# Loading the first chunk of x and base_w ahead of everything else, with the base products started from it, in a two-layer mixer kernel

## The chip, the cores and the metric

The kernel runs on one core of a Trainium2 chip. The metric is the device time of one launch in microseconds (us), as the median over several runs.

## The reference

The input x has 64 samples of 32 channels and 512 positions, float32. Two layers are applied, each one a mix over channels followed by a product along the positions, with the input of the layer added to its result. Cut to what matters for the change:

```python
def layer0(x, cond):                       # x: 64 x 32 x 512, cond: 64 x 128
    h = gelu(cond @ W0 + b0)
    h = gelu(h @ W1 + b1)
    att = softmax(h @ W2 + b2)             # 64 x 8, the mixing network
    agg_w = einsum('bk,koi->boi', att, weight)      # one 32 x 32 matrix per sample
    y = einsum('boi,bih->boh', agg_w, x) + (att @ bias_k)[:, :, None]
    w = softmax of the two largest of (y @ gate_w.T), 0 elsewhere     # 8 experts
    low = einsum('bsd,erd->ebsr', y, lora_A)
    return x + y @ base_w.T + base_b + 2 * einsum('ebsr,eor,bse->bso', low, lora_B, w)

def layer1(x, cond):                       # a grouped convolution of 9 taps, then
    ...                                    # 4 experts, the two best by a router
```

The kernel uses that the mixing matrix and the product along positions act on different axes: it computes x @ base_w.T, x @ lora_A.T and x @ gate_w.T first (they need no mixing matrix) and mixes the products of each tile afterwards.

## The kernel before

**Tiles.** The 64 samples times 32 channels are 2048 rows. They form G = 4 groups of TG = 4 tiles of 128 rows (4 samples each). The 512 positions are DC = 4 chunks of 128; x is stored transposed, so a chunk of x is a 128 x 512 tile `xT_s[:, g % 2, c, :]`, and `wT_s[:, c, :]` (kept in the memory of `x1T`) is the same chunk of base_w.

**Float32 as two parts.** The large products are made in the type fp32r. A tile is split into a high part (ScalarE, ACT: `x_high` L513, `base_high` L598) and a low part, the tile minus its high part. For group 0 and base_w the low parts are VectorE's (DVE: `x_low`, `base_low`, both by `minus` L788), for groups 1 to 3 GpSimd's (POOL: `x_low` L371). `hi_lo` (L1099 to L1101) then makes three products for each pair of chunks: high by high, high by low, low by high.

**Products on TensorE (PE).** `x_base(0, t, chunks)` is x @ base_w.T of tile t of group 0, 3 matmuls of 512 columns for each chunk, added up in the PSUM bank `P0[t]`; all four tiles have a bank of their own. A chunk can be used when its `x_lo` and `base_lo` are there. `x_logits(c)` (L1112) is x @ [lora_A, gate_w] of group 0 in plain float32, four tiles, from the weights `lgw_s`. For groups 1 to 3 `x_first(g, t)` makes these logits and the first 128 columns of the base product in one, 3 matmuls of 264 columns for each chunk.

**Head.** All engines follow an order written out by hand. PE first runs filler products `keep_busy(4, n)` (L1092: n matmuls of 256 columns of ones), then the mixing network in small float32 products (h1 L1338, h2 L1342, the logits of the softmax L1344 and L1347), with more filler between them while ACT makes each gelu (L603, L608) and the exponential (L611). DVE makes the softmax (L947 to L952). PE turns it round (`attT` L1351) and spreads it over tiles (`attb` L1354); `mix_sum` (DVE L792, L796) makes the mixing matrices of a group from `attb` and the weights `wrep_s`, ACT places them into `mixT` (`mix_place` L593), and `mixb` (L1360) gives the bias.

**Routing of group 0.** `mix_logits(0, t)` (PE L1129) mixes the logits of a tile. DVE adds the bias (`logits` L820), then `route0(0)` ranks 8 gates with eleven small operations (`gates`, L768 to L782: `top`, `eq`, `above`, `dif`, `rank`, `kept`, `tot`, `inv`, `w`) and weighs the expert products (`lw` L828). ACT makes the exponential in it (`gate_exp` L556), as soon as `dif` is there; behind it in ACT's order stand `lb_h` (L634, the high part of lora_B) and the four copies `p0_out(0, t)` (L534) that take the base products of group 0 out of PSUM. `x_first(1, t)` writes to the same PSUM bank as `x_base(0, t)` and waits for that copy (`p0_ok`). `turn_lw(0)` (PE L1172) transposes `lw`. Then `make_y(0)` (L1191, `bias_row` L1203, `experts0`) brings the parts of the layer together, and DVE adds them up (L849, L855) into `x1T`.

**Loads.** SP issues early_s (cond, W0, W1, W2, the biases and bias_k), lgw_s, then for each chunk x and base_w of group 0, then group 1 and the rest. ACT issues wrep_s (the mixing weights). POOL's `x_low(1, 2)` waits for `lb_lo`, which DVE gives when it has made the low part of lora_B, behind route0(0).

From there each group's routing, layer 1 of the group before and the products of the next group are interleaved in the same way.

## Time and profile before

| | us |
|---|---|
| median of 3 runs | 176.72 |
| lowest and highest of them | 175.42 and 178.06 |
| the profiled execution, its own time | 177.42 |
| its span, first to last instruction | 175.7 |
| PE busy in the span | 169.9 |
| DVE busy | 125.4 |
| POOL busy | 94.2 |
| ACT busy | 87.1 |

The span begins with the first instruction of any engine; 1.7 us of the execution's own time lie outside it. A time such as 20.92 is counted from the start of the span. Matmuls are pipelined: one row starts before the one ahead of it has ended, so the pace of a run of matmuls is read from start to start. The granted clock of TensorE in the page is in tenths of what the throttle allowed; which of its two levels (1.2 and 2.4 GHz) the engine ran at is read from the pace of equal matmuls.

### The profile page before, as it was taken

The numbers are of one execution on the slowest core, as the hardware profiler recorded it, in microseconds if no ns is written. First come the engines' busy times: TensorE is split into PE (matmuls) and PEld (weight loads), VectorE is DVE, ScalarE is ACT, GpSimd is POOL, SyncE is SP. The second block draws the span as 40 slices with busy tenths as digits, with TensorE's granted clock in tenths as the row PEclk, the third lists the DMA queues.
The fourth block names the chain that finished last, engine by engine and source line by source line (L and its number), as shares of the span: only waits on it lengthen the run. The fifth ranks groups of instructions, "written<-read, shape, count | busy, mean of one in ns | idle before, by whom it ended". The sixth has DMA issues, their size and how long they took to land.

```text
span 175.7 us, 3106 instructions
## 1 busy us (share of the span) xinstructions
PE 169.9 (97%) x1098; PEld 159.1 (91%) x1098; DVE 125.4 (71%) x259; ACT 87.1 (50%) x204; POOL 94.2 (54%) x98
## 2 busy tenths in 40 slices
PE   7999999999999999999999999999999999999990
PEld 7878889999899999998899999999899999999880
DVE  6479199689963559998997336998997954367660
ACT  3864659886453477624251367332315463235231
POOL 8420507999199899936119199730006695066000
PEclk9999999999999999999999999999999999999999
DMA  5999500524001500000032000000041000000336
GB/s 176 237 332 393 202 0 0 194 69 164 14 0 60 168 16 0 4 0 0 0 134 111 0 0 0 4 2 0 15 167 60 0 0 4 2 0 0 122 121 239
DMA packets 7215, 13.21 MB, mean 75 GB/s; under 512 B 800, under 2 KB 1696, under 8 KB 7200
## 3 DMA queue, kind: packets, MB, share of 16 engines
q1 hardware_dynamic: 6768, 12.62, 21.1%
q10 hardware_dynamic: 432, 0.39, 0.7%
q8 instruction: 9, 0.15, 0.4%
q14 instruction: 6, 0.05, 0.1%
HBM read 8.82 MB, written 4.19 MB: 74 GB/s over the span
## 4 chain that ended last, share of the span: by engine, by line
PE 90%; DVE 4%; ACT 2%; issue 1%; POOL 0%; ACTq 0%; DVEq 0%; POOLq 0%
PE ps L1099 21%; PE ps L1101 20%; PE ps L1100 20%; PE ps L1191 8%; PE ps L1092 3%; PE ps L1112 3%; PE ps L1129 2%; PE ps L1288 2%; PE ps L1289 2%; DVE xsl L788 1%; PE ps L1172 1%; PE ps L1300 1%; DVE xs L920 1%; PE ps L1203 1%; PE ps L1330 1%
## 5 line engine op out<-in xcount | busy, mean ns | idle before, releaser
L1099 PE MATMUL ps<-xw_h,xTh 128*128 128x264 f32 (+1 forms) x96 | 30.6, 318 | 0.0
L1100 PE MATMUL ps<-xw_l,xTh 128*128 128x264 f32 (+1 forms) x96 | 29.9, 311 | 0.0
L1101 PE MATMUL ps<-xw_h,xTl 128*128 128x264 f32 (+1 forms) x96 | 29.8, 311 | 0.0
L371 POOL TENSOR_TENSOR xTl<-xT_s,xTh 128x512 fp32r<-128x512 f32 x12 | 15.7, 1333 | 21.1 <-ACT xTh L513 15.7
L376 POOL TENSOR_TENSOR zl<-outb,zh 128x340 fp32r<-128x340 f32 x15 | 15.1, 1007 | 14.9 <-ACT zh L548 7.9
L868 DVE TENSOR_TENSOR outb<-ps,s_sb 128x340 f32<-128x340 f32 x16 | 8.2, 510 | 14.5 <-PE ps L1101 10.8
L1099 PEld LDWEIGHTS ps<-xw_h,xTh 128*128 128x128 f32 x96 | 18.1, 188 | 0.3 <-issue 0.2
L1100 PEld LDWEIGHTS ps<-xw_l,xTh 128*128 128x128 f32 x96 | 18.1, 188 | 0.1
L1101 PEld LDWEIGHTS ps<-xw_h,xTl 128*128 128x128 f32 x96 | 18.1, 188 | 0.0
L1191 PEld LDWEIGHTS ps<-mixT,xp 128*128 128x128 f32 x128 | 16.7, 191 | 1.4 <-DVE x1T L855 0.2
L387 POOL TENSOR_TENSOR x1Tl<-x1T,x1Th 128x512 fp32r<-128x512 f32 x12 | 16.5, 1388 | 2.3 <-DVE late L892 2.3
L855 DVE SCALAR_TENSOR_TENSOR x1T<-ps,side_s,xT_s 128x512 f32<-128x512 f32 x16 | 12.0, 749 | 7.4 <-PE ps L1101 7.2
L1191 PE MATMUL ps<-mixT,xp 128*128 128x128 f32 x128 | 17.1, 276 | 0.0
L548 ACT ACTIVATE zh<-outb 128x340 fp32r<-128x340 f32 x16 | 7.8, 489 | 17.1 <-DVE outb L868 12.4
L387 POOL TENSOR_TENSOR xTl<-x1T,xTh 128x512 fp32r<-128x512 f32 x4 | 6.0, 1502 | 16.6 <-ACT xTh L571 16.5
L849 DVE SCALAR_TENSOR_TENSOR xT_s<-ps,sum_w,xT_s 128x512 f32<-128x512 f32 x16 | 11.6, 742 | 1.5 <-PE ps L1203 1.5
L380 POOL TENSOR_TENSOR zl<-outb,zh 128x272 fp32r<-128x272 f32 x15 | 12.0, 798 | 0.0
L536 ACT ACTIVATE xp<-ps 128x384 f32<-128x384 f32 x12 | 5.8, 490 | 9.7 <-PE ps L1101 9.6
L556 ACT ACTIVATE ex<-dif 128x32 f32<-128x32 f32 (+1 forms) x8 | 1.8, 222 | 17.5 <-DVE dif L771 17.5
L542 ACT ACTIVATE s_sb<-ps 128x340 f32<-128x340 f32 x16 | 7.1, 443 | 6.6 <-PE ps L1101 6.4
L576 ACT ACTIVATE xsh<-xs 128x256 fp32r<-128x256 f32 x12 | 5.0, 417 | 10.0 <-DVE xs L920 5.7
L871 DVE TENSOR_TENSOR outb<-ps,s_sb 128x272 f32<-128x272 f32 x16 | 7.0, 440 | 2.1 <-PE ps L1101 1.9
(232 smaller groups left out, 519.2 us busy)
## 6 DMA issues: line engine op xcount, KB each, us to landing
xT_s<-in_xT_dram SPq DMA_DIRECT2D x16, 256.0 KB, 4.5
out_dram<-outb SPq DMA_DIRECT2D x12, 256.0 KB, 2.3
x1T<-in_wT_dram SPq DMA_DIRECT2D x4, 256.0 KB, 6.8
outb<-in_wrow_dram SPq DMA_DIRECT2D x4, 256.0 KB, 8.1
x1T<-in_az_dram SPq DMA_DIRECT2D x1, 680.0 KB, 9.4
outb<-in_tapw_dram SPq DMA_DIRECT2D x1, 576.0 KB, 3.8
out_dram<-x1T SPq DMA_DIRECT2D x2, 256.0 KB, 2.4
lgw_s<-in_lgw_dram SPq DMA_DIRECT2D x1, 272.0 KB, 3.4
```

Of the source, the lines that this page charges most:

```text
L371: nc.gpsimd.tensor_tensor(lo[:, c, :], xT_s[:, g % 2, c, :], hi[:, c, :].bitcast(F32), ALU.subtract).then_inc(x_lo, 1)
L376: nc.gpsimd.tensor_tensor(zl[:, t, 0:QE, :].rearrange("p k e -> p (k e)"), zf[:, t % 2, 0:NE], zh[:, t, 0:QE, :].bitcast(F32).rearrange("p ...
L380: nc.gpsimd.tensor_tensor(zl[:, t, QE:TAPS, :].rearrange("p k e -> p (k e)"), zf[:, t % 2, NE:NE + NO], zh[:, t, QE:TAPS, :].bitcast(F32). ...
L387: nc.gpsimd.tensor_tensor(lo, full, hi.bitcast(F32), ALU.subtract).then_inc(x1_lo, 1)
L548: nc.scalar.activation(zh[:, t, 0:QE, :].rearrange("p k e -> p (k e)"), zf[:, t % 2, 0:NE], ACT.Copy).then_inc(ze_hi, 1)
L849: nc.vector.scalar_tensor_tensor(out=xT_s[:, i % 2, c, :], in0=ps[:, BROW[i], :], scalar=sum_w[:, c:c + 1], in1=xT_s[:, i % 2, c, :], op0= ...
L855: nc.vector.scalar_tensor_tensor(out=x1T[:, i % 2, c, :], in0=ps[:, Y[c], :], scalar=side_s[:, S_BB + c:S_BB + c + 1], in1=xT_s[:, i % 2, ...
L868: nc.vector.tensor_tensor(zf[:, t % 2, 0:NE], ps[:, ring(t, "U"), 0:NE], s_sb[:, t % 2, :], ALU.add).then_inc(ze_ok, 1)
L1099: nc.tensor.matmul(dst, sh, mh, start=start and c == 0, stop=False)
L1100: nc.tensor.matmul(dst, sh, ml, start=False, stop=False)
L1101: last = nc.tensor.matmul(dst, sl, mh, start=False, stop=stop and c == n - 1)
L1191: nc.tensor.matmul(ps[:, Y[c], cols(t)], p0[:, t, cols(c)], mixer(i, t), start=t == 0, stop=False)
```

## The change

SP loads chunk 0 of x and of base_w first; early_s (without bias_k) and lgw_s follow, then chunk 1, then mixw_s, which holds the mixing weights and bias_k and takes the place of ACT's load of wrep_s. ACT and DVE split chunk 0 ahead of the mixing network and the other chunks between its steps. On PE the products of group 0 with base_w take the place of the filler between the mixing network's products, the first filler grows from 12 to 20 matmuls, and x_first(1) of the chunks 0 and 1 moves ahead of turn_lw(0). On POOL x_low(1, 2) no longer waits for lb_lo.

```diff
             def load_xT(g, c):
                 sp.dma_start(xT_s[:, g % 2, c, :], xT[g, :, c, :]).then_inc(xT_in[g % 2][c], 16)
-            sp.dma_start(early_s[:, :], early).then_inc(in_early, 16)
-            sp.dma_start(lgw_s[:, :, :], lgw).then_inc(in_lgw, 16)
             for c in range(DC):
                 load_xT(0, c)
                 sp.dma_start(wT_s[:, c, :], wT[:, c, :]).then_inc(in_base[c], 16)
+                if c == 0:
+                    sp.dma_start(early_s[:, :], early).then_inc(in_early, 16)
+                    sp.dma_start(lgw_s[:, :, :], lgw).then_inc(in_lgw, 16)
+                elif c == 1:
+                    sp.dma_start(mixw_s[:, :], mixw).then_inc(in_mixw, 16)
...
             pool.wait_ge(base_lo, DC)
-            x_low(1, 0)
-            x_low(1, 1)
-            pool.wait_ge(lb_lo, 1)
-            x_low(1, 2)
-            x_low(1, 3)
+            for c in range(DC):
+                x_low(1, c)
...
-            act.dma_start(wrep_s[:, :, :], wrep).then_inc(in_wrep, 16)
...
-            act.wait_ge(in_early, 16)
+            x_high(0, 0)
+            base_high(0)
+            act.wait_ge(in_lgw, 16)
+            nc.scalar.activation(xw_h[:, :, 0:LG], lgw_s[:, :, :], ACT.Copy).then_inc(lgw_hi, 1)
             act.wait_ge(h1_mm, 1)
             nc.scalar.activation(h1T[:, :], ps[:, HID, 0:NB], ACT.Gelu,
                                  bias=early_s[:, A_B0:A_B0 + 1]).then_inc(h1_ok, 1)
-            act.wait_ge(in_lgw, 16)
-            nc.scalar.activation(xw_h[:, :, 0:LG], lgw_s[:, :, :], ACT.Copy).then_inc(lgw_hi, 1)
+            x_high(0, 1)
             act.wait_ge(h2_mm, 1)
             nc.scalar.activation(h2T[:, :], ps[:, HID, 0:NB], ACT.Gelu,
                                  bias=early_s[:, A_B1:A_B1 + 1]).then_inc(h2_ok, 1)
+            base_high(1)
             act.wait_ge(att_max, 1)
             nc.scalar.activation(att_e[:, :], ps[0:NB, ATT, 0:K0], ACT.Exp, bias=att_m[:, :],
                                  accum_out=att_s[:, :]).then_inc(att_exp, 1)
-            x_high(0, 0)
-            base_high(0)
+            x_high(0, 2)
+            base_high(2)
             act.wait_ge(attT_mm, 1)
             nc.scalar.activation(attT[:, :], attT_b, ACT.Copy).then_inc(attT_ok, 1)
-            for c in range(1, DC):
-                x_high(0, c)
-                base_high(c)
+            x_high(0, 3)
+            base_high(3)
...
             pe.wait_ge(consts, 1)
-            keep_busy(4, 12)
+            keep_busy(4, 20)
+            x_base(0, 0, (0,))
             pe.wait_ge(in_early, 16)
...
-            keep_busy(4, 2)
+            x_base(0, 1, (0,))
...
             nc.tensor.matmul(ps[0:NB, ATT, 0:K0], h2T[:, :], early_s[:, A_W2:A_W2 + K0], start=False, stop=True).then_inc(att_mm, 1)
-            keep_busy(4, 2)
+            x_base(0, 3, (0,))
             x_logits(0)
+            x_base(0, 0, (1,))
+            x_base(0, 1, (1,))
             pe.wait_ge(att_ok, 1)
...
-            keep_busy(4, 3)
+            x_base(0, 2, (1,))
+            x_base(0, 3, (1,))
+            x_logits(1)
...
+            x_logits(2)
+            x_logits(3)
             for t in range(TG):
-                x_base(0, t, (0,))
...
+                x_base(0, t, (2,))
...
             for t in range(TG):
                 mix_logits(0, t)
-            for c in range(2, DC):
-                for t in range(TG):
-                    x_base(0, t, (c,))
+            for t in range(TG):
+                x_base(0, t, (3,))
+            for t in range(TG):
+                x_first(1, t, (0, 1))
             turn_lw(0)
-            for chunks in ((0, 1), (2, 3)):
-                for t in range(TG):
-                    x_first(1, t, chunks)
+            for t in range(TG):
+                x_first(1, t, (2, 3))
             make_y(0)
```

On DVE x_low(0) and base_low(0) move ahead of the low part of lgw, x_low(1) and base_low(1) to either side of the maximum, and x_low(2) and base_low(2) ahead of the first mix_sum; x_low(3) and base_low(3) stay.

PE's first instructions before (L1092 is the filler, L1338 to L1347 the mixing network, L1112 the logits of chunk 0, L1351 and L1354 the turned softmax, L1099 the first product with base_w):

```order
L1092 MATMUL ps<-ones_r 128x256 x12
L1338 MATMUL ps<-early_s 128x64
L1092 MATMUL ps<-ones_r 128x256 x2
L1342 MATMUL ps<-h1T,early_s 128x64
L1344 MATMUL ps<-early_s,ones 64x8
L1092 MATMUL ps<-ones_r 128x256 x2
L1347 MATMUL ps<-early_s,h2T 64x8
L1092 MATMUL ps<-ones_r 128x256 x2
L1112 MATMUL ps<-lgw_s,xT_s 128x136 x4
L1351 MATMUL ps<-ident,att_n 8x64
L1354 MATMUL ps<-att_d,place_r 128x128
L1092 MATMUL ps<-ones_r 128x256 x3
```

and now (L1096 is the filler, L1103 to L1105 the products with base_w, the others the mixing network):

```order
L1096 MATMUL ps<-ones_r 128x256 x20
L1103 MATMUL ps<-xw_h,x1Th 128x512
L1104 MATMUL ps<-xw_l,x1Th 128x512
L1105 MATMUL ps<-xw_h,x1Tl 128x512
L1343 MATMUL ps<-early_s 128x64
L1103 MATMUL ps<-xw_h,x1Th 128x512
L1104 MATMUL ps<-xw_l,x1Th 128x512
L1105 MATMUL ps<-xw_h,x1Tl 128x512
L1347 MATMUL ps<-h1T,early_s 128x64
L1349 MATMUL ps<-early_s,ones 64x8
L1103 MATMUL ps<-xw_h,x1Th 128x512
L1104 MATMUL ps<-xw_l,x1Th 128x512
```

Nine filler matmuls between small products have gone, eight have come at the front, and 12 products with base_w stand between the small ones.

POOL, from the sums over lgw on, before (L371 is x_low of group 1, with what each row waits for):

```order
L396 TENSOR_TENSOR lw<-lgw_s 128x272 [waits in_lgw]
L398 TENSOR_TENSOR lw<-lw 128x136 [waits const_step]
L359 TENSOR_TENSOR xs<-attT,early_s 8x512 [waits attT_ok,in_early]
L371 TENSOR_TENSOR xTl<-xT_s,xTh 128x512 [waits x_hi,base_lo]
L371 TENSOR_TENSOR xTl<-xT_s,xTh 128x512 [waits x_hi]
L371 TENSOR_TENSOR xTl<-xT_s,xTh 128x512 [waits x_hi,lb_lo]
L371 TENSOR_TENSOR xTl<-xT_s,xTh 128x512 [waits x_hi]
```

and now (L378 is the same x_low):

```order
L402 TENSOR_TENSOR lw<-lgw_s 128x272 [waits in_lgw]
L404 TENSOR_TENSOR lw<-lw 128x136 [waits const_step]
L366 TENSOR_TENSOR xs<-attT,mixw_s 8x512 [waits attT_ok,in_mixw]
L378 TENSOR_TENSOR xTl<-xT_s,xTh 128x512 [waits x_hi,base_lo]
L378 TENSOR_TENSOR xTl<-xT_s,xTh 128x512 [waits x_hi] x3
```

The order is the same, but the third and fourth x_low start when ACT has given the high part, no longer when route0(0) is over.

## Rows read from the trace of the kernel before

**Rows 1.** The page, parts 1 and 4: busy time by engine, the chain by engine.
```profile
PE 169.9 (97%) x1098; PEld 159.1 (91%) x1098; DVE 125.4 (71%) x259; ACT 87.1 (50%) x204; POOL 94.2 (54%) x98
...
PE 90%; DVE 4%; ACT 2%; issue 1%; POOL 0%; ACTq 0%; DVEq 0%; POOLq 0%
```

**Rows 2.** Timeline of PE: start us, us, engine line op, out<-in, shapes, count.
```profile
1.24 2.93 PE L1092 MATMUL ps<-ones_r 128*128 128x256 f32 x12 [1.24 <-POOL ones_r L341]
...
10.23 1.01 PE L1092 MATMUL ps<-ones_r 128*128 128x256 f32 x3
11.03 0.63 PE L1099 MATMUL ps<-xw_h,x1Th 128*128 128x512 f32 x1
...
12.72 0.39 PE L1100 MATMUL ps<-xw_l,x1Th 128*128 128x512 f32 x1
...
15.04 3.05 PE L1112 MATMUL ps<-lgw_s,xT_s 128*128 128x136 f32 x24
17.84 0.48 PE L1099 MATMUL ps<-xw_h,x1Th 128*128 128x512 f32 x1
...
20.92 1.09 PE L1129 MATMUL ps<-xp,mixT 128*128 128x136 f32 x8
21.76 0.49 PE L1099 MATMUL ps<-xw_h,x1Th 128*128 128x512 f32 x1
...
27.39 0.60 PE L1172 MATMUL ps<-ident,lw 128*128 128x128 f32 x4
```

**Rows 3.** Timeline of PE from 34 us.
```profile
34.69 0.49 PE L1203 MATMUL ps<-row_b,ones_r 40*128 40x512 f32 x1
```

**Rows 4.** DMA issues between 0.7 and 3.6 us: KB, us from issue to landing.
```profile
early_s<-in_early_dram SPq DMA_DIRECT2D x1, 233.0 KB, 3.0
...
lgw_s<-in_lgw_dram SPq DMA_DIRECT2D x1, 272.0 KB, 3.4
...
x1T<-in_wT_dram SPq DMA_DIRECT2D x1, 256.0 KB, 6.7
```

**Rows 5.** Timeline of SP's queue: start us, us of the issue.
```profile
0.81 0.38 SPq L294 DMA_DIRECT2D early_s<-in_early_dram  x1
1.24 0.42 SPq L295 DMA_DIRECT2D lgw_s<-in_lgw_dram  x1
...
3.13 0.48 SPq L298 DMA_DIRECT2D x1T<-in_wT_dram  x1
```

**Rows 6.** Timeline of ACT.
```profile
6.05 1.28 ACT L611 ACT_TABLE_LOAD   x1
7.35 0.26 ACT L611 ACTIVATE att_e<-ps,att_m 64x8 f32<-64x8 f32 x1
...
21.82 1.14 ACT L513 ACTIVATE xTh<-xT_s 128x512 fp32r<-128x512 f32 x2
...
24.10 0.61 ACT L634 ACTIVATE lb_h<-x1T 128x512 fp32r<-128x512 f32 x1
25.54 2.66 ACT L534 ACTIVATE xp<-ps 128x512 f32<-128x512 f32 x4 [0.82 <-PE ps L1101]
```

**Rows 7.** Timeline of DVE.
```profile
17.31 0.69 DVE L788 TENSOR_TENSOR xw_l<-x1T,xw_h 128x512 fp32r<-128x512 f32 x1
...
22.95 0.41 DVE L769 TENSOR_TENSOR eq<-xp 128x256 f32<-128x256 f32 x1
...
35.28 0.75 DVE L849 SCALAR_TENSOR_TENSOR xT_s<-ps,sum_w,xT_s 128x512 f32<-128x512 f32 x1 [1.50 <-PE ps L1203]
```

**Rows 8.** Timeline of POOL.
```profile
19.32 2.52 POOL L371 TENSOR_TENSOR xTl<-xT_s,xTh 128x512 fp32r<-128x512 f32 x2 [8.12 <-ACT xTh L513]
```

**Rows 9.** Timeline of POOL and of DVE, 77 to 79 us.
```profile
77.09 1.04 POOL L359 TENSOR_TENSOR xs<-attT,early_s 8x512 f32<-8x512 f32 x1 [1.80 <-DVE xsl L788]
...
77.49 0.74 DVE L769 TENSOR_TENSOR eq<-late 128x64 f32<-128x64 f32 x1
78.15 0.21 DVE L770 TENSOR_TENSOR above<-late 128x64 f32<-128x64 f32 x1
```

More of the change, by code:

```diff
@@ L37, with two_layer_mixer @@
 SCALE1 = 16.0 / 16.0 ** 0.5
-A_COND, A_W0, A_W1, A_W2, A_B0, A_B1, A_B2, A_MB, A_N = 0, 64, 192, 320, 328, 329, 330, 338, 466
+A_COND, A_W0, A_W1, A_W2, A_B0, A_B1, A_B2, A_N = 0, 64, 192, 320, 328, 329, 330, 338
+M_W, M_B, M_N = 0, C * K0, C * K0 + P
 S_CTX, S_FS, S_BB, S_N = 0, 128, 129, 133
-def two_layer_mixer(nc: bass.Bass, xT, early, wrep, lgw, wT, wrow, lbT, az, tapw, b1T, side, out):
+def two_layer_mixer(nc: bass.Bass, xT, early, mixw, lgw, wT, wrow, lbT, az, tapw, b1T, side, out):
     with ExitStack() as ctx:
@@ L219, in two_layer_mixer @@
             sem(n) for n in ("consts", "const_step", "ident_ok", "out_act", "place_step", "place_ok", "warm_ok", "zero_ok"))
-        in_early, in_wrep, in_lgw, in_side, in_lb, in_az, in_tap, in_b1 = (
-            sem(f"in_{n}") for n in ("early", "wrep", "lgw", "side", "lb", "az", "tap", "b1"))
+        in_early, in_mixw, in_lgw, in_side, in_lb, in_az, in_tap, in_b1 = (
+            sem(f"in_{n}") for n in ("early", "mixw", "lgw", "side", "lb", "az", "tap", "b1"))
         in_base = [sem(f"in_base{c}") for c in range(DC)]
@@ L1471 @@
     early[0, A_B2:A_B2 + K0] = a["L0_cond_b2"]
-    early[0:K0, A_MB:A_MB + P] = _np.tile(a["L0_cond_bias_k"], (1, BT))
     side = _np.zeros((P, S_N), _np.float32)
@@ L1503 @@
     nc = _bacc.Bacc("TRN2", target_bir_lowering=False, num_devices=1)
-    for name, v in (("xT", xT), ("early", early), ("wrep", wrep), ("lgw", lgw), ("wT", wT), ("wrow", wrow), ("lbT", lbT),
+    for name, v in (("xT", xT), ("early", early), ("mixw", mixw), ("lgw", lgw), ("wT", wT), ("wrow", wrow), ("lbT", lbT),
                     ("az", az.reshape(P, 2, 2, NE)), ("tapw", tapw.reshape(P, TAPS * P)), ("b1T", b1T), ("side", side)):
```

40 lines of the change are left out of this document (20 added, 20 removed).

## The prediction

> **What bounds the kernel now.** I read the page's busy times and its chain first: PE is busy for 169.9 of 175.7 us, and the chain that ended last runs on PE for 90% of the span [rows 1]. So a change counts by what it takes out of PE's own order or by a wait that it puts there. The second view is PE's timeline from the start [rows 2]. The reader is to see in it that PE never idles after 1.24 us, but does two kinds of work that could go. One is filler: 12 matmuls at the start, and nine later. The other is slow work. The 12 filler matmuls of 256 columns took 2.93 us, at most 0.24 each, and the four matmuls of 512 columns from 11.03 to 12.72 are 0.42 us apart: the level of 1.2 GHz. From 12.72 on equal ones are 0.235 us apart (21.76 to 27.39 holds 24), the level of 2.4 GHz. The first useful base product starts only at 11.03.
>
> Then I followed what the moved work meets: the DMA issues [rows 4, 5], ACT's order around the routing [rows 6], and DVE and POOL there [rows 7 to 9].
>
> I cut the head at two points: the start of mix_logits(0), at 20.92, and bias_row(0) inside make_y(0), at 34.69. The parts that they end took 20.92 and 13.77 us. What happens at the second point moves the end of the kernel one for one, as long as no other engine becomes late behind it.
>
> **First part, up to mix_logits(0).** After the change PE has this to do: 36 base matmuls (chunks 0 to 2), 16 logit products, the small products, and no filler once chunk 0 is there.
> - The base matmuls at the high level: 36 x 0.235 = 8.5.
> - The logits: 12 products took 17.84 - 15.04 = 2.8, so 16 take 3.7.
> - The small products (mixing network, turned softmax, mixb, sum of lgw) and the changes between kinds: before, from the end of the first filler (1.24 + 2.93 = 4.2) to 10.23 it is 6.0 us. Six fillers (6 x 0.24 = 1.4) and four logit products at the low level (twice 0.23 each, 1.9) are in it, which leaves 2.7. mixb and the sum of lgw add some 0.6, and the high level takes part of it back: an estimate of 2.7 (2.2 to 3.3).
> Sum 14.9. When does it start? x takes early_s's place in SP's queue and base_w that of lgw_s. Those landed at 0.81 + 3.0 = 3.8 and 1.24 + 3.4 = 4.6 [rows 4, 5]. Behind base_w's landing stand its high part (0.61, as the copy of lora_B of the same shape [rows 6]) and its low part (0.69 [rows 7]), so 5.9. The 20 filler matmuls last until 1.24 + 20 x 0.24 = 6.0, or less if the clock rises in them, so they cover just this. All at the high level, mix_logits(0) would start at 5.9 + 14.9 = 20.8.
>
> **The clock.** No row shows this order. In the rows 12 dense matmuls at the start were not enough, the small products between fillers did not help, and the level rose 2.5 us after dense work had begun again at 10.23 [rows 2]. After the change dense work is never far: 4.6 us of filler, then three large matmuls for each small product. I expect the rise between 4.6 and 8.5 and take 7.0, which costs half of 7.0 - 5.9, 0.5. If it stayed low until 12.7 as before, it would cost half of 6.8, 3.4. So the first part ends at 21.3 (20.8 to 24.2); it gains nothing by itself, but one more chunk of base products (12 matmuls, 2.8) is behind us by then than before.
>
> **Waits that could open there.** Chunk 1 of base_w was issued at 3.13 and landed at 9.8 [rows 4, 5]; fewer bytes stand ahead of it now. Its two parts add 1.3: usable at 11.1, and PE comes to it at about 11.2. Between them lies nothing, so up to 0.5 is possible. The exponential now has base_high(1) ahead of its table load. The load took 1.28, and the exponential began 1.30 after the load's start [rows 6]; behind base_high(1), which ends at 10.4, that is 11.7. PE wants the softmax at 12.5, which leaves 0.8 for the exponential (0.26) and three small DVE operations: nothing, or 0.2 at most. The Trainium skill, ScalarE: Activation LUTs, section What ACT_TABLE_LOAD costs, counts some 2.66 us for a switch of tables, load and drain together. By that the exponential would begin at 13.1, PE would wait some 1.2 us and the sum below would rise by that much; the row above contradicts it, and I go by the row. The first mixing matrices move behind base_low(2) on DVE, by some 2 us, and PE's mix_logits(0) comes last of all in this part, behind 24 base products that cover that.
>
> **Second part, mix_logits(0) to bias_row(0).** It took 34.69 - 20.92 = 13.77 [rows 2, 3]. The moved chunk leaves: -2.8. Two waits come.
> - x_first(1, 0) now comes right behind the last base products, 0.84 + 2.8 = 3.65 after mix_logits(0) starts. It needs p0_out(0, 0), and in ACT's order that stands behind gate_exp and lb_h. Those ended at 24.7 [rows 6], 3.8 after mix_logits(0), and the copy takes 0.62 more: 4.4. A wait of 0.75. The next copies are 0.66 apart and PE needs 0.73 for each tile, so it is paid once. Before, nobody saw it, since PE was busy with base products until 27.39 (a lower bound of 0.75).
> - POOL. Its x_low(1, 2) and (1, 3) now start when ACT has given the high parts, the first at 22.5 on the old scale [rows 6], and last 1.26 each [rows 8], until 25.0. In these 2.5 us DVE runs eq and, right behind it, above of the gates; eq used to start at 22.95 and took 0.41, with POOL idle [rows 7]. Where a POOL operation lay beside eq, eq took 0.74, although it ended just after POOL's operation did and its like (above, same shape) took 0.21 [rows 9]. So eq should be held until 23.75, and above possibly until 25.0, and dif, the exponential and all of p0_out with them: 0.8 in one case, 1.7 in the other. I take 1.3. Nothing hides it, since PE already waits there.
> The Trainium skill, SBUF — State Buffer, section SBUF: two separate sides, says that a VectorE operation with two SBUF inputs and a GpSimd operation exclude each other for the whole instruction. By that rule both delays come in full, and the total rises by 0.4 over mine.
> So the second part is 13.77 - 2.8 + 0.75 + 1.3 = 13.0. turn_lw(0) ran without a wait 6.5 after mix_logits(0) (27.39 - 20.92 [rows 2]), so lw is there by 7.8 even with the delay, and turn_lw(0) is now wanted at 8.6 or later: no wait.
>
> **Sum.** 21.3 + 13.0 = 34.3 against 34.69: 0.4 gained. The profiled execution took 177.42; 177.42 - 0.4 = 177.0. The median of the runs shown is 0.7 below the profiled one. So the forecast is 0.3 above that median, and with runs from 175.42 to 178.06 that is no change one can see. 2% of the time, 3.5 us, is about what a measurement of this kernel can tell from no change.
>
> **What is late next.** DVE's bias addition started at 35.28 and waited 1.50 for bias_row(0) [rows 7]. So DVE's path from mix_logits(0) to there was 33.8 - 20.9 = 12.9 and is now 14.2 with the POOL delay, so it arrives 1.2 behind bias_row(0) at 13.0. make_y needs its first result 2.8 after bias_row(0), and DVE needs 1.4 for the pair, so this fits with about 0.2 to spare; later pairs are 1.6 apart on PE and 1.4 on DVE.
>
> **Rivals.**
> 1. *POOL does not hold DVE.* Its operations fall between DVE's, or the high parts come late. For it: the window is narrow, 2.5 us, and shifts if POOL is late. Against: rows 9. Then the second part is 11.7, with the clock up by 5.9 the point is at 32.5, and the time 177.42 - 2.2 = 175.2 (175.7 with the clock at 7.0).
> 2. *The low clock lasts (slower).* Small products and first waits for x keep PE from being dense enough, and it rises only near 12.7. For it: filler from 1.24 to 3.96 did not raise it, and x or base_w may land after the filler ends. Against: the rise came 2.5 us after 10.23 with no denser work. Then 24.2 + 13.0 = 37.2, and 177.42 + 2.5 = 179.9. It decides for slower from a rise later than about 8 us (7.0 + 0.8).
> 3. *DVE or ACT becomes the bound behind bias_row(0).* The spare of 0.2 is used up and mix_logits(1), turn_lw(1) follow DVE. For it: DVE has work without a gap from mix_logits(0) to there. Against: PE needs more for each chunk than DVE. Price: up to 1.2, the time 178.2.
> 4. *The change does not start early*: x lands later than early_s did, because it is now the first and larger transfer. PE then waits between filler and chunk 0. Against: early_s had nearly the same size (233 KB) and landed in 3.0. A wait of 1 us gives 178.0.
>
> **How the numbers follow.** Forecast (177.0, give or take 1): 0.48. Rival 1: 0.22. Rival 2: 0.13. Rivals 3 and 4: 0.12. The rest, 0.05, is something unseen downstream in either direction. The range reaches down to rival 1 with the spread of the runs, 174.7, and up to most of rival 2, 179.3. Only the far ends of these cases pass 2% from 176.72 (173.2 and 180.3): faster 0.05, same 0.88, slower 0.07.
>
> **What would show it.** Right: matmuls of 512 columns at 0.235 apart from about 7 us on; mix_logits(0) at 21 to 21.5; PE idle some 2 us ahead of the first 264-column matmul, released by ACT's copy of the base products; eq and above of the first gates taking over 0.8 together; bias_row(0) at 34.3. Wrong: base products still 0.42 apart beyond 9 us, no idle time at x_first(1, 0), or a new wait of PE between 35 and 60 us.

## The result, and the profile after

The changed kernel took 183.63 us (median of 6 runs, 180.58 to 185.23), the kernel before 175.8 beside it (6 runs, 175.06 to 178.06). The ratio is 1.033, 95% interval 1.028 to 1.039: slower. The forecast was 177.0 with a range up to 179.3, and no change as the likeliest case: wrong. The profiled execution of the changed kernel took 182.5 with a span of 180.8, that of before 177.42 with 175.7, so 5.1 us can be followed row by row. One thing is needed to read the numbers: the ratios leave out runs over 1.5% above the fastest of their kernel (three of the changed kernel's six, so 1.033 stands where the two medians would give 1.045), and the runs of the kernel before lie in two groups, near 175.3 and near 177.6, with the profiled one in the upper group.

The page of the changed kernel, parts 1, 2 (the granted clock in 40 slices) and 4, against [rows 1]:
```profile
PE 169.8 (94%) x1097; PEld 158.9 (88%) x1097; DVE 125.3 (69%) x259; ACT 86.6 (48%) x204; POOL 94.0 (52%) x98
...
PEclk9979999699999999999999999999999999999998
...
PE 83%; DVE 7%; ACT 3%; DMA 3%; issue 1%; SPq 0%; ACTq 0%; DVEq 0%
```
PE's busy time is unchanged, 169.8 against 169.9, and the span is 5.1 longer. So PE waits now, and where it works slower, other work has gone to balance it. PE's share of the chain fell from 90% to 83%, and DMA (3%), DVE and ACT have the rest. The clock row has two dips, a 7 and a 6: one in the first part, one behind 31 us. (PEclk is the granted clock in tenths.)

PE's timeline of the changed kernel (start us, us, engine line op, tiles, shapes, count, idle time before and its releaser), against [rows 2, 3]:
```profile
1.24 4.27 PE L1096 MATMUL ps<-ones_r 128*128 128x256 f32 x20 [1.24 <-POOL ones_r L348]
...
4.99 0.52 PE L1096 MATMUL ps<-ones_r 128*128 128x256 f32 x3
8.35 0.77 PE L1103 MATMUL ps<-xw_h,x1Th 128*128 128x512 f32 x1 [2.84 <-DVE xw_l L792]
...
10.62 0.63 PE L1104 MATMUL ps<-xw_l,x1Th 128*128 128x512 f32 x1
11.05 0.63 PE L1105 MATMUL ps<-xw_h,x1Tl 128*128 128x512 f32 x1
...
12.42 0.40 PE L1104 MATMUL ps<-xw_l,x1Th 128*128 128x512 f32 x1
12.66 0.39 PE L1105 MATMUL ps<-xw_h,x1Tl 128*128 128x512 f32 x1
...
24.66 1.09 PE L1133 MATMUL ps<-xp,mixT 128*128 128x136 f32 x8
...
30.79 0.39 PE L1103 MATMUL ps<-xw_h,xTh 128*128 128x264 f32 x1 [2.28 <-ACT xp L536]
...
32.12 0.33 PE L1104 MATMUL ps<-xw_l,xTh 128*128 128x264 f32 x1
32.24 0.42 PE L1105 MATMUL ps<-xw_h,xTl 128*128 128x264 f32 x1
32.46 0.42 PE L1103 MATMUL ps<-xw_h,xTh 128*128 128x264 f32 x1
...
35.10 0.87 PE L1176 MATMUL ps<-ident,lw 128*128 128x128 f32 x4
...
39.74 0.49 PE L1207 MATMUL ps<-row_b,ones_r 40*128 40x512 f32 x1
```
The reader is to see four things (the second row is a part of the first). The filler ends at 5.51 and the first base product comes at 8.35: 2.84 of idle time. The last three filler matmuls start 0.12 apart, where those before 4.6 are 0.21 apart, so the 2.4 GHz level was there from about 4.9 on. Behind the idle time it is gone: base products are 0.43 apart, the 1.2 GHz level, until about 12.0, and 0.24 apart after it. mix_logits(0) starts at 24.66 (20.92 before). Then PE waits 2.28 for ACT's copy of the base products, and shortly after, the 264-column matmuls go from 0.12 apart to 0.22 apart until 35.9: a second stretch at the low level. bias_row(0) starts at 39.74 instead of 34.69. From there on the two kernels run 5.05 us apart to the end, so everything lies in these 40 us.

The DMA issues of the first 2.6 us (KB, us from issue to landing), against [rows 4]:
```profile
lgw_s<-in_lgw_dram SPq DMA_DIRECT2D x1, 272.0 KB, 5.9
xT_s<-in_xT_dram SPq DMA_DIRECT2D x1, 256.0 KB, 4.1
x1T<-in_wT_dram SPq DMA_DIRECT2D x1, 256.0 KB, 5.6
early_s<-in_early_dram SPq DMA_DIRECT2D x1, 169.0 KB, 5.7
```
x was issued at 0.81 and landed at 4.9, base_w's chunk at 1.24 + 5.6 = 6.8. early_s and lgw_s, which took 3.0 and 3.4 in first place, take 5.7 and 5.9 behind them. Behind base_w's landing stand 1.5 us of high and low part (1.3 forecast): 8.35.

DVE's and POOL's timelines around the first gates, against [rows 7, 8]:
```profile
26.69 1.14 DVE L773 TENSOR_TENSOR eq<-xp 128x256 f32<-128x256 f32 x1
27.75 1.49 DVE L774 TENSOR_TENSOR above<-xp 128x256 f32<-128x256 f32 x1
```
```profile
26.25 2.71 POOL L378 TENSOR_TENSOR xTl<-xT_s,xTh 128x512 fp32r<-128x512 f32 x2 [0.70 <-ACT xTh L515]
```
The starts of eq, above and dif (29.28) are 2.59 apart in sum, where before they were 0.79 apart: 1.8 more, and POOL's two subtractions (26.25 to 28.96) lie beside them.

Stretches of the changed kernel: length, then busy time (and count) of PE, PEld, DVE, ACT and POOL, then the granted clock, the DMA share and GB/s:
```profile
8.00:10.00 2.00, 1.65 (x5) 1.40 (x6) 0.93 (x2) 0.66 (x1) 1.62 (x2) 0.58 1.05 402
10.00:12.00 2.00, 2.00 (x9) 1.64 (x8) 0.69 (x1) 0.85 (x3) 0.00 (x0) 0.56 1.06 407
12.00:14.00 2.00, 2.00 (x11) 1.42 (x11) 0.71 (x2) 1.98 (x3) 0.00 (x0) 1.00 1.05 389
28.00:32.00 4.00, 1.72 (x12) 1.29 (x11) 3.76 (x9) 2.50 (x6) 0.96 (x1) 1.00 0.00 0
32.00:36.00 4.00, 4.00 (x23) 4.00 (x22) 3.86 (x5) 0.20 (x1) 2.47 (x2) 0.57 0.00 0
```
and one of the kernel before:
```profile
10.00:12.00 2.00, 2.00 (x8) 1.58 (x8) 1.43 (x2) 2.00 (x5) 1.04 (x1) 1.00 0.98 295
```
Both slow stretches of the changed kernel show in the granted clock: 0.58 and 0.56 from 8 to 12, and 0.57 behind 32 us, behind a stretch in which PE was busy for 1.72 of 4 us. The slow start of the kernel before does not: its matmuls are 0.42 apart there too, and the granted clock is 1.00. So there are two different things here, a level that has not risen yet, which only the pace of equal matmuls tells, and a level that was up and is taken back, which both tell. The changed kernel has the second kind twice. In the row of 32 to 36 us DVE's and ACT's operations have their usual lengths; it is PE that is slow.

### The profile page after: what moved, and what is told of

The parts are those of the page before. It is cut to its first block, busy times and chain, and to the rows that moved or that the text cites. A ratio compares the mean times of both kernels' runs of the same rounds, so it can differ in the third digit from the quotient of the medians.

```text
span 180.8 us, 3103 instructions
## 1 busy us (share of the span) xinstructions
PE 169.8 (94%) x1097; PEld 158.9 (88%) x1097; DVE 125.3 (69%) x259; ACT 86.6 (48%) x204; POOL 94.0 (52%) x98
## 4 chain that ended last, share of the span: by engine, by line
PE 83%; DVE 7%; ACT 3%; DMA 3%; issue 1%; SPq 0%; ACTq 0%; DVEq 0%
PE ps L1103 20%; PE ps L1105 19%; PE ps L1104 19%; PE ps L1195 8%; DMA x1T<-in_wT_dram 3%; PE ps L1116 2%; PE ps L1133 2%; PE ps L1292 2%; PE ps L1293 2%; PE ps L1176 1%; DVE xsl L792 1%; PE ps L1304 1%; DVE xs L924 1%; DVE eq L773 1%; PE ps L1207 1%
## 5 line engine op out<-in xcount | busy, mean ns | idle before, releaser
L1103 PE MATMUL ps<-xw_h,xTh 128*128 128x264 f32 (+1 forms) x96 | 31.2, 325 | 2.3 <-ACT xp L536 2.3
L1105 PE MATMUL ps<-xw_h,xTl 128*128 128x264 f32 (+1 forms) x96 | 30.6, 318 | 0.0
L1104 PE MATMUL ps<-xw_l,xTh 128*128 128x264 f32 (+1 forms) x96 | 30.5, 317 | 0.0
L378 POOL TENSOR_TENSOR xTl<-xT_s,xTh 128x512 fp32r<-128x512 f32 x12 | 15.4, 1306 | 13.3 <-ACT xTh L515 13.3
L1103 PEld LDWEIGHTS ps<-xw_h,xTh 128*128 128x128 f32 x96 | 18.6, 194 | 3.0 <-ACT xp L536 2.7
L1104 PEld LDWEIGHTS ps<-xw_l,xTh 128*128 128x128 f32 x96 | 18.6, 194 | 0.1
L1105 PEld LDWEIGHTS ps<-xw_h,xTl 128*128 128x128 f32 x96 | 18.7, 195 | 0.0
L366 POOL TENSOR_TENSOR xs<-attT,mixw_s 8x512 f32<-8x512 f32 x4 | 4.2, 1042 | 15.3 <-ACT attT L621 7.1
L1103 PE MATMUL ps<-xw_h,x1Th 128*128 128x512 f32 x16 | 7.7, 479 | 2.8 <-DVE xw_l L792 2.8
```

The lines of the kernel that those rows point to most:

```text
L378: nc.gpsimd.tensor_tensor(lo[:, c, :], xT_s[:, g % 2, c, :], hi[:, c, :].bitcast(F32), ALU.subtract).then_inc(x_lo, 1)
L1103: nc.tensor.matmul(dst, sh, mh, start=start and c == 0, stop=False)
L1104: nc.tensor.matmul(dst, sh, ml, start=False, stop=False)
L1105: last = nc.tensor.matmul(dst, sl, mh, start=False, stop=stop and c == n - 1)
```

## The experiments

Two points cut the head as in the prediction. All values are from the profiled execution of each kernel, the median and the ratio from its timed runs beside the kernel before on the same chip. "First" is the first base product, "part 1" ends with mix_logits(0), "part 2" is from there to bias_row(0). What an edit brings is read from the spans and the ratios.

| kernel | base_w chunk 0 lands | first | part 1 ends | part 2 | bias_row(0) | median us | ratio to before (95%) |
|---|---|---|---|---|---|---|---|
| before | 7.9 | 11.03 | 20.92 | 13.77 | 34.69 | 175.8 | |
| changed | 6.8 | 8.35 | 24.66 | 15.08 | 39.74 | 183.63 | 1.033 (1.028 to 1.039) |
| e1_contig | 4.1 | 5.66 | 20.91 | 15.06 | 35.97 | 177.77 | 1.013 (1.009 to 1.018) |
| e2_p0first | | 8.37 | 27.26 | 12.06 | 39.32 | 183.6 | 1.043 (1.037 to 1.049) |
| e3_poolwait | | 8.03 | 25.80 | 13.10 | 38.90 | 181.74 | 1.036 (1.032 to 1.040) |
| e4_filler36 | | 8.01 | 22.77 | 13.52 | 36.29 | 179.97 | 1.025 (1.020 to 1.030) |
| e5_contig_p0 | | 5.75 | 20.94 | 12.07 | 33.01 | 177.56 | 1.008 (1.005 to 1.012) |
| e6_before_contig | | 9.45 | 18.65 | 13.77 | 32.42 | 175.21 | 0.998 (0.994 to 1.003) |
| e7_contig_p0_early | | 5.78 | 21.18 | 10.98 | 32.16 | 175.77 | 0.998 (0.994 to 1.002) |
| e8_before_loads | | 14.74 | 24.99 | 13.77 | 38.76 | 180.33 | 1.024 (1.018 to 1.031) |
| e9_after_oldloads | 8.1 | 9.59 | 27.80 | 15.04 | 42.84 | 184.98 | 1.046 (1.040 to 1.053) |
| e10_xcontig | 5.6 | 7.16 | 23.55 | 15.07 | 38.62 | 179.59 | 1.022 (1.017 to 1.026) |
| e11_contig_poolwait | | 5.61 | 20.64 | 13.09 | 33.73 | 176.67 | 1.006 (1.003 to 1.009) |
| e12_all_poolwait | | 5.59 | 20.52 | 15.21 | 35.73 | 178.01 | 1.012 (1.006 to 1.018) |

### e1_contig: chunk 0 lands late because its rows lie apart

In the stored x and base_w a chunk's 128 rows of 2 KB lie 8 KB apart. Here each chunk is one piece of 256 KB; nothing else changes.
```diff
-                sp.dma_start(xT_s[:, g % 2, c, :], xT[g, :, c, :])
+                sp.dma_start(xT_s[:, g % 2, c, :], xT[g, c, :, :])
-                sp.dma_start(wT_s[:, c, :], wT[:, c, :])
+                sp.dma_start(wT_s[:, c, :], wT[c, :, :])
```


> The changed kernel with x and base_w stored in DRAM chunk by chunk, so that each load of a chunk reads 256 KB in one piece and no longer 128 rows that stand 8 KB apart; nothing else differs. Theory A (the first loads from x and base_w are slow because their rows are scattered over 1 MB that nobody has read yet): x lands about 3.0 us after its issue instead of 4.1 and base_w after 3.4 instead of 5.6, chunk 0 starts at about 6 instead of 8.35, and the time falls by 2 to 3 us against the changed kernel, to about 180. Theory B (whatever is loaded first is slow, because the DMA engines start up): both land as in the changed kernel, at 4.9 and 6.8, and the time is that of the changed kernel, about 182.5.

The DMA issues of the first 2.6 us of this kernel:
```profile
lgw_s<-in_lgw_dram SPq DMA_DIRECT2D x1, 272.0 KB, 4.6
xT_s<-in_xT_dram SPq DMA_DIRECT2D x1, 256.0 KB, 2.7
x1T<-in_wT_dram SPq DMA_DIRECT2D x1, 256.0 KB, 2.9
early_s<-in_early_dram SPq DMA_DIRECT2D x1, 169.0 KB, 3.0
```
PE's timeline of it:
```profile
5.66 0.47 PE L1103 MATMUL ps<-xw_h,x1Th 128*128 128x512 f32 x1 [0.40 <-DVE xw_l L792]
```
The same bytes in the same order land 1.4 (x), 2.7 (base_w and early_s) and 1.3 (lgw_s) sooner. The first base product comes at 5.66, within 0.3 of the 5.9 of the forecast; base products are at 0.24 from the start, and the first part ends at 20.91 (forecast 20.8 with the clock up at once). The span falls by 3.8 (180.8 to 177.0) and the ratio from 1.033 to 1.013. That is more than the 2 to 3 us of the first theory, because with only 0.40 of idle time before chunk 0 the level was not lost either. So the late landing is the largest single cause, and it is the layout in memory that makes it. The second part, with its idle time of 2.28 and the low level from 28.45 to 32.16, stands unchanged at 15.06: a separate cause. The low stretch does not come in every execution: this profiled run has a mean granted clock of 0.985 and a span of 177.0, the three other runs have 0.993 to 1.000 and spans of 175.7 to 176.1.

### e2_p0first: ACT's copies ahead of the exponential
```diff
+            for t in range(TG):
+                p0_out(0, t)
             gate_exp(0, gate0, dif0_ok, ex0_ok)
             ...
-            for t in range(TG):
-                p0_out(0, t)
             lwT_high(0)
```


> The changed kernel with ACT's four copies p0_out(0, t) ahead of gate_exp(0) and lb_h. Theory A (PE's idle time before x_first(1, 0), and the low clock that follows it, come from the place of the copies in ACT's order): PE goes from the last base product at 28.1 straight on to the 264-column matmuls, no matmul at the low level between 32 and 35.5, and turn_lw may wait up to 1 us for lw; the time falls by 3 to 4 us, to about 179. Rival (the routing chain of DVE sets bias_row(0) anyway): the idle time only moves to turn_lw or make_y, and the time falls by less than 1 us.

The idle time ahead of the first 264-column matmul is gone, and no stretch at the low level follows. The second part fell from 15.08 to 12.06. All waits of PE in this kernel (engine, tile, line, waited for, in total, times, longest):
```profile
PE ps L1103 <- DVE xw_l L792: 2.5, 1, 2.5
PE ps L1195 <- DVE x1T L859: 1.3, 1, 1.3
...
PE ps L1176 <- DVE lw L832: 0.8, 1, 0.8
```
The place of the idle time was taken by two others that DVE sets, 0.8 before turn_lw and 1.3 before mix_base: with POOL still holding it, DVE is the next bound. The total, 183.6, shows none of the 3.0 gained, since in this kernel base products stayed 0.43 apart until 17.7 and the first part ended at 27.26. Here the level had never risen before: all 20 fillers were slow (4.63 us, 4.27 in the changed kernel), and the granted clock is 1.00 all the way. The edit touches nothing ahead of mix_logits(0), so I put that down to the clock and not to the edit; no run tests it. Neither this nor the total tells the edit's worth; e5 does.

### e3_poolwait: POOL waits for lb_lo again
```diff
-            for c in range(DC):
-                x_low(1, c)
+            x_low(1, 0)
+            x_low(1, 1)
+            pool.wait_ge(lb_lo, 1)
+            x_low(1, 2)
+            x_low(1, 3)
```


> The changed kernel with POOL's wait for lb_lo ahead of x_low(1, 2) put back. Theory A (POOL's two operations held eq and above of the gates): eq and above take 0.41 and 0.42 again instead of 1.14 and 1.49, the idle time before x_first(1, 0) shrinks from 2.3 to about 0.5, but x_first(1, t) of chunks 2 and 3 waits 1 to 1.5 us for POOL; the time falls by 1 to 2.5 us, to about 180.5. Rival (eq and above are long for another reason): they stay at 1.1 and 1.5, and the time rises by the wait for POOL, to about 184.

eq and above took 0.41 and 0.42 again, and the idle time fell from 2.28 to 0.48: POOL's part of it is 1.8. No low stretch follows. New waits of 0.2 and 0.6 for POOL's low parts come instead, and the second part is 13.10. The first part (25.80) again depends on the clock: behind an idle time of 2.16 base products were at the high level from 8.03 to about 9.3 and then at the low one until 16.1, with a granted clock of 0.50.

### e4_filler36: filler until chunk 0 is there
```diff
-            keep_busy(4, 20)
+            keep_busy(4, 36)
```


> The changed kernel with 36 filler matmuls at the start instead of 20, so that PE has no idle time before chunk 0 comes. Theory A (the idle 2.8 us before chunk 0 kept the clock low until 11.9): the high level is there when chunk 0 starts at about 8.4 to 9, and mix_logits(0) comes 1 to 2 us earlier, the time is about 181. Rival (the rise depends on something else, or the filler only delays): the filler ends near 9.0, mix_logits(0) moves later by 0.6 and the time is about 183.

PE's timeline of this kernel:
```profile
5.67 2.49 PE L1096 MATMUL ps<-ones_r 128*128 128x256 f32 x16
8.01 0.47 PE L1103 MATMUL ps<-xw_h,x1Th 128*128 128x512 f32 x1
8.32 0.40 PE L1104 MATMUL ps<-xw_l,x1Th 128*128 128x512 f32 x1
8.56 0.39 PE L1105 MATMUL ps<-xw_h,x1Tl 128*128 128x512 f32 x1
```
Without the idle gap the level rose at about 6.6 and stayed: the first part took 22.77 - 8.01 = 14.76 from the first base product, the forecast's 14.9; in the changed kernel it took 16.31. The span fell by 3.2 (180.8 to 177.6), the ratio from 1.033 to 1.025. The wait of 2.28 before x_first(1, 0) is here too, but no low stretch follows it in this execution, and that makes the second part 13.52 instead of 15.08. So a low stretch in the second part costs 1.56. It is not the filler that keeps it away: two of this kernel's four runs have a mean granted clock of 0.999 and 1.000 and a span of 177.6, the other two 0.985 and 0.986 and spans of 178.8 and 179.0, so they very likely had it.

### e5, e6, e7: contiguous rows, then the waits one by one

e5 is e1 and e2 together.

> The changed kernel with both x and base_w stored chunk by chunk and the four copies p0_out(0, t) ahead of gate_exp(0). Theory (the two waits are independent, and DVE is the next bound behind them): mix_logits(0) at about 20.9 as with the contiguous loads alone, the part from there to bias_row(0) falls from 15.1 to about 12.1, and some 1.5 us come back as waits of PE for x1T between the blocks of make_y(0), as DVE's work still holds POOL's delay of 1.8; time about 176.3. Rival (the clock decides alone): no fall against the contiguous loads alone, about 177.8, with low-clock stretches in the record.

Part 2 is 12.06 and 12.07 in the two kernels with this edit, so the order of the copies brings 3.0 with the low stretch, 1.5 without it (13.52 - 12.06). bias_row(0) comes at 33.01, 2.96 before e1's, and yet the span is only 1.2 shorter (175.8 against 177.0) and the median 0.2: the kernel no longer follows this point one for one, and the time comes back behind it, 1.3 of it in a wait for DVE's x1T. Against the runs of e1 without a low stretch (175.7 to 176.1) its spans of 175.5 to 176.0 gain nothing, and the 176.3 expected was missed by 1.3.

e6 is the kernel before with the contiguous rows of e1 and nothing else.

> The kernel before with x and base_w stored chunk by chunk, nothing else. Theory (before, the loads of chunk 0 are hidden behind the mixing network and the filler, so their speed does not matter): the same time as the kernel before within 0.5%, with x landing in about 3 us. Rival (they do bound the head, or free the DMA engines for what follows): 1 us or more faster.

```profile
6.50 1.09 PE L1112 MATMUL ps<-lgw_s,xT_s 128*128 128x136 f32 x8
...
9.45 0.47 PE L1099 MATMUL ps<-xw_h,x1Th 128*128 128x512 f32 x1 [0.20 <-DVE xw_l L788]
```
This is PE's timeline of it. The kernel before gains nothing from the layout (ratio 0.998, the first theory): its PE works on early_s, lgw_s and filler until 9.45, and chunk 0 was there in time anyway. The eight logit products at 6.50 take 1.09, the high level, which the profiled execution of before had only from 12.7 on. With it this kernel's mix_logits(0) starts at 18.65, 2.3 before the 20.92 that I started from, and its span is 173.4. That is the difference between the two groups of runs of the kernel before (175.3 and 177.6), as far as sizes can tell; no second profile of before was taken.

e7 is e5 with DVE's mix_sum(2) ahead of logits(0, t), and ACT's x_high(1, 0) and (1, 1) ahead of mix_place(0), (1, 2) and (1, 3) behind xl_out(1), so that POOL is done before DVE compares.
```diff
             base_low(3)
+            dve.wait_ge(base_lo, DC)
+            mix_sum(2, prods[1], TG, TG)
             for t in range(TG):
                 logits(0, t)
...
             base_high(3)
+            x_high(1, 0)
+            x_high(1, 1)
             act.wait_ge(zero_ok, 1)
```


> The kernel e5 and in addition: DVE makes the mixing matrices of group 1 (mix_sum(2)) ahead of the logits of group 0, where it was idle, and ACT makes the high parts of x of group 1 earlier (chunks 0 and 1 ahead of mix_place(0), 2 and 3 ahead of the sum over lgw), so that POOL is through with x_low(1) before the gates begin. Theory (POOL's delay of eq and above and DVE's work behind the routing are the last two costs): eq and above take 0.4 each, no idle time of PE between x_first(1, 0) and mix_logits(1), bias_row(0) at about 31.8, the time about 173, that is 1 to 2% faster than the kernel before. Rival (DVE or ACT is late elsewhere): 175 or more.

DVE's timeline around its gates, and the two longest of PE's waits behind its head:
```profile
23.21 0.55 DVE L773 TENSOR_TENSOR eq<-xp 128x256 f32<-128x256 f32 x1
23.68 0.41 DVE L774 TENSOR_TENSOR above<-xp 128x256 f32<-128x256 f32 x1
```
```profile
PE ps L1268 <- DVE late L896: 0.4, 1, 0.4
PE ps L1103 <- DVE outb L872: 0.4, 1, 0.4
```
With POOL out of the way PE has no wait before bias_row(0), which comes at 32.16, the earliest of all. But that is only 0.26 ahead of e6. (At most 0.5 more is the clock: this execution's base products were slow until about 6.6, and its first part took 15.40 from the first of them, 14.93 in e12.) PE's products from the first base product to there are the same in any order, and what the early start replaces is filler. Behind it e7 loses 1.5 against e6 (spans of 174.6 and 173.4). These two waits for DVE are 0.8, but e6 has 0.2 of the first one too, so they explain 0.6; another 0.2 is a wait for POOL, and the rest was not followed. The total equals the kernel before's (ratio 0.998, 0.994 to 1.002), and the 173 expected was missed: the rival held. This is what the change is worth when all that it stumbles over is removed.

### e8 and e9: the order of the loads and the order of the work, one at a time

e8 is the kernel before with x and base_w chunk 0 issued ahead of early_s and lgw_s; e9 is the changed kernel with early_s and lgw_s first.
```diff
-            sp.dma_start(early_s[:, :], early).then_inc(in_early, 16)
-            sp.dma_start(lgw_s[:, :, :], lgw).then_inc(in_lgw, 16)
             for c in range(DC):
                 load_xT(0, c)
                 sp.dma_start(wT_s[:, c, :], wT[:, c, :]).then_inc(in_base[c], 16)
+                if c == 0:
+                    sp.dma_start(early_s[:, :], early).then_inc(in_early, 16)
+                    sp.dma_start(lgw_s[:, :, :], lgw).then_inc(in_lgw, 16)
```


> The kernel before with SP's first four loads in the order of the change (chunk 0 of x, of base_w, early_s, lgw_s), scattered as they are, PE and the others in the old order. Theory (the scattered first loads hold up what stands behind them in the queue): early_s lands near 7.4 instead of 3.8, the mixing network begins 3.5 us later with PE idle before it, mix_logits(0) comes 3 to 4 us later, the time is about 179. Rival (the order of the loads costs nothing by itself, since the loads share the DMA engines): early_s lands near 5, the time is within 1.5 us of the kernel before.

> The changed kernel, with early_s and lgw_s put back ahead of x and base_w in SP's queue (rows as in the changed kernel, mixw_s still behind chunk 1). The instruction orders of PE, ACT, DVE and POOL stay as changed. Theory A (the first scattered loads are slow to land wherever they stand, and what counts is what PE can do meanwhile): x chunk 0 lands about 6.1 us and base_w chunk 0 at about 7.8, as in the kernel before; PE ends its 20 fillers near 5.5, waits for the base product until about 9.1 to 9.4 (0.8 later than in the changed kernel), and since h1 stands behind that product in PE's order, early_s and lgw_s landing early bring nothing: total 183 to 184.5, no better than the changed kernel. Theory B (the place of early_s and lgw_s behind x is what costs, because the mixing network is late): the total falls by 1 us or more below the changed kernel's, to 180 to 182. In both, the waits of 2.28 before x_first(1, 0) and eq / above of 1.14 / 1.49 us stay as they are.

One row of PE's timeline of each, first e8, then e9:
```profile
7.54 0.69 PE L1339 MATMUL ps<-early_s 128*128 128x64 f32 x2 [3.38 <-DMA early_s<-in_early_dram]
```
```profile
9.59 0.77 PE L1102 MATMUL ps<-xw_h,x1Th 128*128 128x512 f32 x1 [3.72 <-DVE xw_l L791]
```
The load order alone makes the kernel before 2.4% slower (1.8 to 3.1): its mixing network waits 3.38 for early_s. The work order alone, with the old loads, makes it 4.6% slower: PE has nothing to do but chunk 0, and that lands at 8.1. So the new work order needs the new load order, and with it pays 3.3% all the same. e9 came out much as the first theory of its text had it: the first base product came at 9.59 (9.1 to 9.4 expected), and its runs spread from 182.83 to 186.72 around the 183 to 184.5 expected.

### e10_xcontig: x or base_w

Only x is stored chunk by chunk here (the first pair of lines of e1's diff).

> The changed kernel with x alone stored chunk by chunk (its loads are contiguous 256 KB); base_w's rows stay 8 KB apart (2 KB each). Theory A (each tensor's first rows are slow by themselves): x lands at about 3.5 us after the start, base_w chunk 0 still not before 5.5 to 6.5, so the first base product comes at 7 to 7.8, half of the way to the 5.66 of the form with both contiguous, and the total is 179 to 181. Theory C (only x, the first of the queue, holds up everything behind it): base_w lands at about 4.2, first base product at 5.7, total as with both contiguous, 177.4 to 178.7. Theory D (base_w alone sets it): first base product stays at 8.3 and the total at 182 to 184.

```profile
xT_s<-in_xT_dram SPq DMA_DIRECT2D x1, 256.0 KB, 2.7
x1T<-in_wT_dram SPq DMA_DIRECT2D x1, 256.0 KB, 4.4
```
In these rows of its DMA issues x lands in 2.7 as in e1, base_w in 4.4, between 5.6 and 2.9. The first base product comes at 7.16, the total is 179.59, both within what the first theory gave: each tensor's scattered rows cost by themselves, some 1.2 us for x and 1.5 for base_w.

### e11 and e12: does the clock's second fall come from the idle time?

e11 is e1 with POOL's wait of e3.

> The changed kernel with x and base_w stored chunk by chunk, and POOL's wait for lb_lo between x_low(1, 1) and x_low(1, 2) put back. It differs from the contiguous form only in what POOL runs beside DVE's eq and above. Theory A (POOL's subtraction holds DVE's comparison, and the idle time of 2.28 before x_first(1, 0) is what lets the granted clock fall): eq / above 0.41 / 0.42, the idle time there 0.5 instead of 2.28, no stretch at the low level after it (in the form without the wait it lasts from 28.45 to 32.16), second part 12.5 to 13.2 instead of 15.06, bias_row(0) at 33.4 to 34.2, total 175.6 to 176.8. Theory B (the fall of the clock there has another cause): the low stretch appears all the same, second part 14 to 15, total 177 to 178.

DVE's gates and the two longest of PE's waits behind the first base product:
```profile
22.67 0.41 DVE L776 TENSOR_TENSOR eq<-xp 128x256 f32<-128x256 f32 x1
23.00 0.42 DVE L777 TENSOR_TENSOR above<-xp 128x256 f32<-128x256 f32 x1
```
```profile
PE ps L1106 <- POOL xTl L378: 0.8, 2, 0.6
PE ps L1106 <- ACT xp L539: 0.5, 1, 0.5
```
Everything fell within the first theory's numbers: the idle time is 0.48, there is no low stretch, part 2 is 13.09, the total 176.67. The first part is that of e1 to 0.3. So POOL's subtractions hold DVE, and without the long idle time the clock stays up. That does not rest on one profile: none of the 29 runs of e5, e7 and e11, whose idle times behind the first base product are 1.3 at most, has a mean granted clock below 0.993.

e12 puts everything together: e11 with p0_out first (e2) and mix_sum(2) early (e7's DVE edit), without e7's moves on ACT.

> The changed kernel with all of its waits in the head taken away and nothing else moved: x and base_w stored chunk by chunk, p0_out(0, t) ahead of gate_exp(0) on ACT, mix_sum(2) ahead of logits(0, t) on DVE, and POOL's wait for lb_lo put back (instead of the x_high moves of e7_contig_p0_early, which lost 1.3 us again behind the head). Theory A (the change moves PE's work only; with no wait left it equals the contiguous form of the kernel before): eq / above 0.41 / 0.42, no idle time of PE over 0.3 us before mix_base, bias_row(0) at 32 to 32.6, total 174.8 to 175.8, same. Theory B (the earlier start of the base products is worth something once nothing waits): bias_row(0) below 31.9 and total below 174.6. Theory C (DVE is now the bound behind the head, as in e7): bias_row(0) at 32 to 32.6 but the total 176 or more.

All three theories were wrong: 178.01. One row of POOL's and one of PE's timeline tell why:
```profile
27.49 3.00 POOL L378 TENSOR_TENSOR xTl<-xT_s,xTh 128x512 fp32r<-128x512 f32 x2 [6.06 <-DVE lb_l L795]
```
```profile
29.30 0.39 PE L1106 MATMUL ps<-xw_h,xTh 128*128 128x264 f32 x1 [1.57 <-POOL xTl L378]
```
The wait for lb_lo that spares DVE's comparison now comes too late: PE reaches the tile that needs POOL's low parts before POOL has begun them, since lb_h stands behind four copies on ACT and lb_l behind lw on DVE. Idle times of 1.57 and 0.61 follow, and behind them again a low stretch from 31.8 until about 35. A wait restored from the kernel before is right only while the rest of the order is that of before.

## Why the prediction was wrong

**When chunk 0 is usable (the step that failed).** The prediction took x's and base_w's landing from early_s and lgw_s, because they stood at those places of the queue (3.8 and 4.6, usable at 5.9). They landed at 4.9 and 6.8, usable at 8.35: +2.45, of which 2.2 is base_w's landing and 0.2 its two parts. The same view held a row for base_w's chunk 1 with 6.7 us, and in the same trace its chunk 0 took 5.7. I read these as time spent behind other transfers. e1, e9 and e10 show that most of it goes with the layout. Rival 4 (x lands later) had the wait in the right place, but for another reason (the first and larger transfer), with 1 us and with 0.12 shared with another case.

**What it does to the clock.** The forecast was a single rise at 7.0, for 0.5 us. In the trace the level was up already at about 4.9, in the filler; it was lost behind the 2.84 of idle time and came back near 12.0, some 3.7 us after the first base product. From that product to mix_logits(0) the changed kernel took 16.31, and 14.76 at the high level (e4), so the low level cost 1.55 instead of 0.5. The prediction had no term for a level that is lost again behind a wait: its reason, that dense work is never far, fell with the idle time. Rival 2 had nearly the cost, but a different mechanism, a level that does not rise until late; that one is seen in e2. The work itself was sized right: 14.9 forecast, 14.76 in e4. The first part ended at 24.66 where 21.3 was forecast, and 2.45 + 1.05 - 0.14 = 3.36 is all of it.

**Waits in the first part.** Chunk 1 and the softmax made none, as forecast. The table load at 12.83 took 1.28 and the exponential began at 14.13, 1.30 after it, as in the row of before; of the further drain that the Trainium skill, ScalarE: Activation LUTs, section What ACT_TABLE_LOAD costs, counts, this trace shows nothing either.

**p0_out behind the exponential.** Right in place, and with POOL's part of 1.8 taken from 2.28 it is 0.48, where 0.75 was forecast (e3, e11).

**POOL against eq and above.** Right in mechanism, 1.3 forecast, 1.8 measured; the bound of 1.7 was the right end. e3, e7 and e11 confirm it: with POOL's work out of the way eq took 0.41 (0.55 in e7, where POOL ended 0.3 us into it) and above 0.41 or 0.42. The rule of the Trainium skill, SBUF — State Buffer, section SBUF: two separate sides, that the two exclude each other for the whole instruction, agrees: by it the total would have been 0.4 higher than mine, and the trace shows 0.5 more.

**The second fall of the clock (not foreseen).** With the waits as they were, part 2 would be 13.52 (e4; forecast 13.0). The low stretch behind the idle time adds 1.56; it is the same loss as in the first part, met again, and by e1's and e4's runs it does not come in every execution. Sum of the misses at bias_row(0): 3.36 + 0.5 + 1.56 = 5.4, from the 34.3 forecast to the measured 39.74.

**What is late next.** DVE did become the bound once ACT's order was mended (e2, e5), by 0.8 and 1.3, and waits for it are a part of what e7 loses again. In the changed kernel itself it was not, since PE was later still.

**The reference.** The sum was made against a profiled execution with a late clock. In the other group of its runs the kernel before is 2 us faster, so even the forecast of 0.4 gained stood on a good comparison only for one group. e6 against e7 gives the fair one: 0.26 at bias_row(0), 0.7 at most with e7's slow start taken off, and nothing in the total.

## What to carry to other kernels

Price a transfer by the row of that very transfer, its shape and layout included, and not by the row of whatever stood at its place in the queue. Before work is moved to the front, ask what covers its data's arrival if that is 2 us late: here the filler and the mixing network had been this cover, and giving them up cost the wait and the clock with it. Read the clock twice, from the granted clock and from the pace of equal matmuls; the first alone does not show a slow start. A wait that an order takes away may have kept two engines from blocking each other; look at which operations of DVE and POOL will lie side by side, and when a wait is put back, check it against the new order.
